# Routing inside the attention loop, scattered rows and scatter-added results in place of a sort and a dense part, and a register wait for each tile's expert weights

## What is computed

```python
x = x + tanh(g_xattn) * xattn(layernorm(x), ctx, ...)   # 16 heads of 64, one shared k and v; softmax; @Wo;
                                                        # plus silu(gate) * h @ Wff2 with h, gate = xn @ Wff1
x = x + tanh(g_ffn) * ffn(layernorm(x), ...)

# ffn: the shared expert, and the best 2 of 8 experts for each token, of width 256 and hidden size 256
shared = silu(x @ sh_up_w + sh_up_b) @ sh_down_w + sh_down_b
scores = softmax(xf @ gate_w.T)
topk_w, topk_i = top_k(scores, 2); topk_w = topk_w / (topk_w.sum() + 1e-20)
h = silu(einsum('nd,edh->neh', xf, up_w) + up_b)
y = sum over the token's two experts of topk_w * (h @ down_w + down_b)
```

## Time and profile before

| | us |
|---|---|
| runs of the kernel before | 632.3, 631.11, 632.21 (median 632.21) |
| span of the profiled execution, first to last instruction | 629.7 |
| busy in the span: PE, DVE, ACT, POOL | 550.9, 447.8, 343.6, 237.9 |

### The profile page before, as it was taken

The page is one execution under the profiler, slowest core; times in us unless marked ns, Lnnn a source line. Parts: engine busy times, 40 slices in busy tenths (PEclk is TensorE's granted clock), DMA queues, the critical chain, the costliest instruction groups (busy, mean ns, idle before and its releaser), DMA issues.

```text
span 629.7 us, 13343 instructions
## 1 busy us (share of the span) xinstructions
PE 550.9 (87%) x4099; PEld 522.0 (83%) x4100; DVE 447.8 (71%) x1176; ACT 343.6 (55%) x1108; POOL 237.9 (38%) x254
## 2 busy tenths in 40 slices
PE   1779999999999999999999999998477999995175
PEld 1778999999999999999999999987477999984175
DVE  7767878778778878778877876768997445551057
ACT  2467656756666756665766665776603444531042
POOL 3355523323323333332342342354626444127600
PEclk9989999999999999999999999999859999997568
DMA  4550200100100100000100000005202333323303
GB/s 144 164 179 30 84 2 1 36 0 0 33 0 0 33 0 0 33 0 0 33 0 0 0 17 1 2 18 168 69 18 83 119 117 115 86 75 102 108 1 133
DMA packets 26691, 31.54 MB, mean 50 GB/s; under 512 B 2947, under 2 KB 24388, under 8 KB 26660
## 3 DMA queue, kind: packets, MB, share of 16 engines
q1 hardware_dynamic: 23244, 22.88, 11.2%
q0 software_dynamic: 3088, 8.27, 4.8%
q10 hardware_dynamic: 330, 0.02, 0.0%
HBM read 22.61 MB, written 8.55 MB: 49 GB/s over the span
## 4 chain that ended last, share of the span: by engine, by line
PE 68%; DVE 15%; ACT 5%; issue 5%; another core or an unknown queue 5%; DMA 0%; DVEq 0%; POOL 0%; ACTq 0%; SPq 0%
PE bank L1325 21%; PE bank L1326 19%; PE bank L1327 19%; PE bank L1459 4%; PE bank L1522 2%; DVE xn L847 2%; ACT pr L647 1%; PE bank L1653 1%; PE bank L1645 1%; DVE acts L1018 1%; ACT acts L622 1%; DVE xs L1301 1%; ACT weights L695 1%; DVE q_t L1086 1%
## 5 line engine op out<-in xcount | busy, mean ns | idle before, releaser
L507 POOL TENSOR_TENSOR pr<-pr,rden 128x512 f32<-128x512 f32 x64 | 66.7, 1042 | 161.2 <-DVE rden L1013 161.0
L1325 PE MATMUL bank<-acts,weights 128*128 128x256 f32 x384 | 110.6, 288 | 5.8 <-DVE weights L895 2.9
L1327 PE MATMUL bank<-acts,weights 128*128 128x256 f32 x384 | 109.8, 286 | 0.0
L1326 PE MATMUL bank<-acts,weights 128*128 128x256 f32 x384 | 109.6, 286 | 0.0
L647 ACT ACTIVATE pr<-bank,nmax 128x128 f32<-128x128 f32 x256 | 90.4, 365 | 28.1 <-DVE nmax L984 27.1
L1325 PEld LDWEIGHTS bank<-acts,weights 128*128 128x128 f32 x384 | 74.8, 195 | 10.2 <-issue 4.0
L1325 PE MATMUL bank<-weights,acts 128*128 128x256 f32 x256 | 80.5, 314 | 2.1 <-POOL acts L512 2.0
L512 POOL TENSOR_TENSOR acts<-uf,acts 128x256 fp32r<-128x256 f32 x64 | 47.1, 736 | 83.1 <-ACT acts L639 83.1
L1326 PEld LDWEIGHTS bank<-acts,weights 128*128 128x128 f32 x384 | 74.5, 194 | 2.4
L955 DVE TENSOR_TENSOR acts<-bank,acts 64x256 fp32r<-64x256 f32 x128 | 53.9, 421 | 30.1 <-ACT acts L622 29.3
L1327 PEld LDWEIGHTS bank<-acts,weights 128*128 128x128 f32 x384 | 74.5, 194 | 0.0
(11 more groups left out here) (248 smaller groups left out, 1630.6 us busy)
## 6 DMA issues: line engine op xcount, KB each, us to landing
slot_rows<-stage SPq DMA_DIRECT2D x35, 128.0 KB
ct<-in_ctx SPq DMA_DIRECT2D x8, 256.0 KB, 2.7
xs<-in_x SPq DMA_DIRECT2D x8, 256.0 KB, 4.8
spare<-in_L_xattn_Wff SPq DMA_DIRECT2D x8, 256.0 KB, 4.4
norm_rows<-xn SPq DMA_DIRECT2D x7, 256.0 KB, 2.2
out_x<-xs SPq DMA_DIRECT2D x3, 512.0 KB, 3.0
stage<-in_L_xattn_Wff SPq DMA_DIRECT2D x2, 512.0 KB, 4.4
stage<-in_L_xattn_Wo SPq DMA_DIRECT2D x2, 512.0 KB, 5.0
```

The costliest lines, as they stand in the source:

```text
L507: pool.tensor_tensor(pr[:, s % 2], pr[:, s % 2], rden[:, s % 2, :].unsqueeze(2).broadcast_to((P, 4, P)), ALU.mult).then_inc(probs_ready, 1)
L1325: pe.matmul(ps, wts[1], mov[0], start=first, stop=False, skip_group_check=True)
L1326: pe.matmul(ps, wts[0], mov[0], start=False, stop=False, skip_group_check=True)
L1327: return pe.matmul(ps, wts[0], mov[1], start=False, stop=last, skip_group_check=True)
```

## The change

Routing moves into the attention loop, one group behind, for all eight groups. For each group DVE finds the best two experts (max, max_index), PE counts choices within the group (count_choices), and DVE adds running counts per expert (taken) to give each of the token's two copies a row in its expert's region of slot_rows. POOL scatters the normalised rows there, each with two more columns, the token's number and the choice's weight: first choices at the end of the iteration, second choices at s = 1 of the next but one. X1T moves from s = 5 to s = 3, GL from s = 7 to s = 5. The last group takes the same way in the bridge. SP fills 640 rows past each expert's count with pad rows in the last iteration, ahead of the last two groups' rows.

All four steps of the shared expert run before the tiles, and SP stores their sums to the output. There are 39 tiles. SP loads each with plain DMAs, its first row from a register. PE waits in each tile for ring_ready to reach the tile's expert number plus 2, a value in a register, and no longer for all splits before tile 0. DVE multiplies a tile's result by its weights, and POOL adds it to the output rows in DRAM by an indirect DMA with addition. Scatter t waits for that of t-2, and for that of t-1 where tile t has another expert or is past the last filled tile (a count from a table, in a register). The dense part, norm_rows, the stores and the fetching back go. The bias rows are no longer padded with zeros to 128 rows.

```diff
-MIX_MID = ["FF0", "QP2", "FF1", "FF2", "QP3", "FF3", "FF4", "FF5", "X1T", "TXc", "FF6", "GL", "FF7",
+MIX_MID = ["FF0", "QP2", "FF1", "FF2", "QP3", "FF3", "X1T", "FF4", "GL", "FF5", "TXc", "FF6", "FF7",
            "TXx"] + NEXT
-MIX_LAST = [n for n in MIX_MID if n not in ["TXc", "TXx"] + NEXT]
+MIX_LAST = [n for n in MIX_MID if n not in ["TXc", "TXx"] + NEXT] + ["RK"]
...
-NTS = NB - 2
-NCH = 2 * NTS
-TILES = NCH + NE - 1
+TILES = 2 * NB + NE - 1
...
@@ SP
+            for e in range(NE):
+                first = sp.value_load(start_at[0:1, e:e + 1], min_val=0, max_val=PAD_ROW - AHEAD)
+                sp.dma_start(slot_rows[bass.ds(first, AHEAD)].rearrange("(a p) n -> p a n", p=P),
+                             pad_row.unsqueeze(1).broadcast_to((P, AHEAD // P, ROW))).then_inc(pads_stored, 16)
...
+            def load_tile(t, slot_of):
+
+                row = sp.value_load(tile_row[0:1, bass.ds(t, 1)], min_val=0, max_val=PAD_ROW)
+                sp.dma_start(rows_g[:, slot_of, :], slot_rows[bass.ds(row, P), 0:D]).then_inc(gathered[slot_of], 16)
+                sp.dma_start(meta[:, bass.ds(t, 1), :].rearrange("p a n -> p (a n)"), slot_rows[bass.ds(row, P), D:ROW]
+                             ).then_inc(gathered[slot_of], 16)
...
+            sp.wait_ge(tables_done, 1)
+            sp.wait_ge(first_routed, 32 * (NG + 1))
+            sp.wait_ge(second_routed, 32 * (NG + 1))
...
@@ POOL
+            def send(rows, c, done):
+
+                for t in range(2):
+                    pool.indirect_dma_start(slot_rows[:, :], bass.IndirectOffsetOnAxis(ap=slot[:, 2 * t + c:2 * t + c + 1], axis=0),
+                                            rows[:, t, :], None).then_inc(done, 16)
+
+            def second_rows(g, rows):
+
+                pool.wait_ge(first_routed, g * 32 + 64)
+                pool.sem_inc(send_steps, 1)
+                pool.tensor_copy(rows[:, :, D + 1], w_second).then_inc(weight_moved, 1)
+                pool.wait_ge(weight_moved, g + 2)
+                pool.sem_inc(send_steps, 1)
+                send(rows, 1, second_routed)
+
+            def first_rows(g, rows):
+
+                pool.wait_ge(slots_done, g + 1)
+                pool.wait_ge(token_done, g + 2)
+                pool.sem_inc(send_steps, 1)
+                send(rows, 0, first_routed)
...
+                    if s == 1 and not first:
+                        second_rows(g - 2, xrow)
...
+            expert_lo(2)
+            second_rows(NG - 2, xrow)
+            for c in range(3, 6):
                 expert_lo(c)
-            for c in range(5, NPOS - 1):
+            pool.wait_ge(slots_done, NG)
+            send(xrow_last, 0, first_routed)
+            expert_lo(6)
+            second_rows(NG - 1, xrow_last)
+            for c in range(7, NPOS):
                 expert_lo(c)
...
+            pool.wait_ge(written, 16 * TPS)
+            for t in range(TILES):
+                pool.wait_ge(y_copied, t + 1)
+                if t >= 1:
+                    due = pool.value_load(turn[0:1, t:t + 1], min_val=16, max_val=16 * (TILES // 2 + 2))
+                    pool.wait_ge(y_added[t % 2], 16 * (t // 2) + 16)
+                    pool.wait_ge(y_added[(t - 1) % 2], due)
+                else:
+                    pool.wait_ge(y_added[0], 16)
+                    pool.wait_ge(y_added[1], 16)
+                pool.indirect_dma_start(out_rows, bass.IndirectOffsetOnAxis(ap=meta[:, t, 0:1].bitcast(I32), axis=0),
+                                        ys[:, t % 4, :], None, compute_op=ALU.add).then_inc(y_added[t % 2], 16)
...
@@ DVE
-                    if s > 1:
+                    if s > 1 or s == 0 and not first:
                         small_step()
...
+                    if s == 3 and not first:
+
+                        dve.wait_ge(second_routed, g * 32)
+                        norm_apply(call, x_tiles(g - 1), xrow[:, :, 0:D], 4, x1norm_done)
+                    if s == 4 and not first:
+                        x1_lo(g - 1, mix_ps[mix_bank("X1T", g, first, last)]).then_inc(mix_freed, 1)
...
                         dve.scalar_tensor_tensor(u1[:, :], th[:, :], 1.0, b[:, GT:2 * GT], ALU.add, ALU.mult
                                                  ).then_inc(u1_done, 1)
+                        if s == 1 or s == 2 or s == 0 and not first:
+                            small_step()
...
-                    if s in (1, 2, 3):
+                    if s in (1, 2, 3) or s == 0 and not first:
                         small_step()
...
+            def best_logits(n):
+
+                for t in range(2):
+                    done = dve.max(top[:, t, :], lgt[:, t, :])
+                done.then_inc(route_step, 1)
...
+            def token_ranks(b):
+
+                dve.tensor_tensor(rank, b[:, 0:2 * NE].rearrange("p (t e) -> p t e", t=2),
+                                  taken.unsqueeze(1).broadcast_to((P, 2, NE)), ALU.add)
+                return dve.tensor_copy(added, b[:, 2 * NE:3 * NE])
...
                     if isinstance(t, int):
+                        n, weight = t - 2, meta[:, t - 2, 1:2]
                         if t >= 6:
-                            dve.wait_ge(y_stored[b], 16 * ((t - 2) // 4))
+                            dve.wait_ge(y_added[b % 2], 16 * (n // 2))
...
-                    dve.tensor_copy(ys[:, b, :], bank[6 + c % 2][:, 0:D]).then_inc(y_copied, 1)
...
+                    dve.tensor_scalar(ys[:, b, :], bank[6 + c % 2][:, 0:D], weight, None, ALU.mult).then_inc(y_copied, 1)
...
@@ PE
+            def turn_logits(b, src):
+
+                for t in range(2):
+                    done = pe.transpose(b[:, GT + t * NE:GT + (t + 1) * NE], src[:, t * P:(t + 1) * P], ident[0:NE, 0:NE])
+                done.then_inc(lt_filled, 1)
+
+            def count_choices(b, n):
+
+                pe.wait_ge(chosen_done, n + 1)
+                pe.matmul(b[:, 0:3 * NE], before, chosen, start=True, stop=False, skip_group_check=True)
+                pe.matmul(b[:, NE:3 * NE], ones, chosen[:, 0:2 * NE], start=False, stop=False, skip_group_check=True)
+                return pe.matmul(b[:, 2 * NE:3 * NE], ones, chosen[:, 0:NE], start=False, stop=True,
+                                 skip_group_check=True)
...
+                            if i == 1 and s == 5 and not first:
+                                pe.wait_ge(lgt_done, g)
...
-                    if s == 5 and not first:
+                    if s == 3 and not first:
                         b = mix("X1T", g, first, last)
                         pe.wait_ge(x1norm_done, g)
-                        transposes(b, xn[:, 0:2]).then_inc(mix_filled, 1)
+                        transposes(b, xrow).then_inc(mix_filled, 1)
...
                 if loop is None and t == 0:
-                    for n in range(NE):
-                        split(pe, NCA + 1 + n)
                     pe.wait_ge(brow_in, 32)
-                    pe.wait_ge(windows_done, 1)
+                    pe.wait_ge(tables_done, 2)
...
                     e = pe.snap((experts_of >> (SHIFT * (k + 2))) & (NE - 1))
+                    pe.wait_ge(ring_ready, e + 2)
...
```

More of the change, by code:

```diff
@@ L581, in _ @@
+            for i in range(2):
+                pool.wait_ge(y_added[i], 16 * len(range(i, TILES, 2)) + 16)
         @block.scalar
@@ L656, in iteration @@
                         probs_hi(u - 1, first and s == 1)
+                    if s == 4 and not first:
+                        act.wait_ge(mix_filled, mix_index("X1T", g, first, last) + 1)
+                        act.activation(gates_in[:, 0:1], gates[:, 0:1], ACT.Copy)
+                        x1_hi(g - 1, mix_ps[mix_bank("X1T", g, first, last)])
                     if s < NU:
@@ L1032, in iteration @@
                                                  ).then_inc(mix_freed, 1)
-                    if s == 5 and not first:
-                        x1_lo(g - 1, mix_ps[mix_bank("X1T", g, first, last)]).then_inc(mix_freed, 1)
+                    if s == 7 and not first:
+                        choice_weights(g - 1, xrow)
                     if s == 0:
@@ L1442, in iteration @@
                         done.then_inc(mix_filled, 1)
+                    if s == 5 and not first:
+                        turn_logits(gl, lgT)
                     if s == 0:
```

900 lines of the change are left out of this document (416 added, 484 removed).

## The result

The change makes the kernel slower. The changed kernel takes 659.89 us (median of four runs, 658.63 to 663.66) where the kernel before, run beside it, takes 631.66: ratio 1.0452, 95% interval 1.0411 to 1.0494. I had forecast 607 and put 0.17 on slower. The profiled execution took 658.63, of which the span is 656.8.

The account below looks back on a forecast made before the run. PE was taken to bound the attention loop and expert tiles, DVE the bridge, nothing the dense part. From 632.2, minus 71.3, plus 17.3, 4.9, 11.3 and about 12 for the scatters' tail gave 607 us; range 583 to 636.

Parts of the forecast that it names:

- What bounds the kernel now: Whole kernel before: PE bounds attention loop and expert tiles, DVE's sorting chain the bridge, no engine the dense part.
- little slack: Attention loop: DVE and ACT form a ring of dependent work nearly as long as PE's slot.
- the 71.3 us that I booked as removed: End of the kernel before, 558.4 to 629.7: dense part and fetching back, stalled stretch included, all counted as saved.
- The attention loop, 2.5 us an iteration: Attention loop: growth per iteration from added PE work and three stalls, bounds 0.5 to 4.5, 17.3 us in all.
- The bridge, E+56: Attention to sorted tiles: tiles start 56 us after E, the end of attention, against 51.1 before; net +4.9.
- The tiles, 2.245 us each: Expert tiles: PE's pace per tile; 39 rather than 35 tiles add 9.0 us.
- the register wait: PE's ring_ready wait in each tile: 0.06 us each, 2.3 us over 39 tiles, bounds 0 and 8.
- The scatter-adds, L = 4.0: Tile stage: L is us from start to landing; 49 halves of L make a 98 us chain that binds, ending at 604.5.
- long scatters: Rival, tile stage: scatter-adds cost a read and a write in turn, L of 6.35, giving 665 us; chance 0.13.
- Slow loop: Rival, attention loop: it grows by 4.5 us an iteration, giving 621 us; chance 0.12.
- Starved code: Rival, leaving the tile loop: engines crawl during back-to-back scatter-adds, some 25 us more, giving 632 us; chance 0.08.
- PE binds: Rival, tile stage: with L under 3.6 scatter-adds keep up and PE sets the time, 596 to 599 us; chance 0.24.

Follow-up runs that it names:

- e1: The changed kernel with bias rows again zero-padded to 128 rows and full bias matmuls: 648.91 us, ratio 1.0269 to the kernel before.
- e2: The changed kernel with one constant wait for all split weights ahead of tile 0 instead of a register wait in each tile: 663.65 us, ratio 1.0485.
- e8: The kernel of e1 with plain indirect stores in place of scatter-adds, sums of shared part and experts left out of the output: 630.81 us (one run).
- e10: The kernel before with one indirect store from POOL to scratch after DVE's last addition: 612.16 us beside 606.95, ratio 1.0098.
- e9: The kernel before with only the changed kernel's two-row bias matmuls: 633.39 us beside 606.95, ratio 1.0409.
- e4: The kernel before with four unused indirect stores to scratch added to POOL in each attention iteration: 632.43 us beside 631.05, ratio 1.001.
- e13: The changed kernel with full bias matmuls, later loop steps and counting matmuls, up to four scatter-adds in flight: 624.58 us, ratio 1.0279 to the kernel before at 606.79.
- e14: The kernel of e13 with the two sends of second choices in different slots: 622.44 us, ratio 1.0251 to the kernel before at 606.79.
- e3: The changed kernel with norm steps and x1's transposes at their old places, logits one slot later, counting matmuls unmoved: 675.46 us.
- e15: The kernel before with its 32 indirect fetches at the end two at a time instead of back to back: 638.28 us beside 630.91, ratio 1.0117.

## Why the prediction was wrong

*What bounds the kernel now.* Right, and the loop's "little slack" was the reading that mattered. But the dense part's stalled stretch, among the 71.3 us that I booked as removed, is not a fixed property: at the other level the kernel before is 24 us shorter, and 19 us of PE's "issue" waits are not there. At that level the change loses 54 us, not 28.

*The attention loop, 2.5 us an iteration: mis-sized.* It grew by 5.1. Each of the three places that I named did stall: uf (0.8, and 1.1 for the pT behind it), X1T (1.9, as computed), the wait for X1T to be freed (1.0). I had the parts right and then took "one stall gives back part of the next". They added up, past even my upper bound of 4.5. My reading is that DVE starts each slot from PE's scores, so that a wait of PE delays DVE's next work too and gives it nothing back; no run shows this by itself. I had also costed nothing for the clock: in the iteration from 305.33 it was 0.97 and PE's work 51.26 us, where the one before it had 1.00 and 49.90, and so in three of seven. Over the loop, 38.3 us came where 17.3 were forecast (7 x 2.5 is 17.5; a slip of no weight).

*The bridge, E+56: right* (56.5). After it I counted 6 us to the first scatter-add. It was 10.3, at a granted clock of 0.66, with PE busy in 10.36 of 10.40 us: I had priced the first tile at the full clock.

*The tiles, 2.245 us each: the step that left something out, and the main one that failed.* I read in the diff that the bias rows are no longer padded, and costed nothing for it. It is 0.38 us a matmul, 78 times here, and puts PE at 2.86 us a tile. In the changed kernel PE and the scatter-adds are nearly equal bounds: PE is busy 103.85 of 104.90 us, though the chain without PE's delay takes 108 of the 113.8 (e1). That is why e1 gives 10 us and not the 30 that 78 times 0.38 would be. For the register wait I allowed 2.3 us; e2 shows none.

*The scatter-adds, L = 4.0: a part left out.* I had L from start to landing, and that was sized well: 3.6 to 3.8 us. But each step of the chain also holds the 0.75 us from the landing to POOL's next issue, which I had put at nothing, so a step is 4.41 to 4.62. The count of halves holds from first to last issue: e1's chain is 48 of them at 2.25. I had counted 49 to the landing of the last, which gave that landing half an L (2.0 us); it took 3.6. So the 19.5 us too many from the first scatter-add to the last landing are 12.0 of the longer step, 5.8 of PE's late tiles and some 1.6 of that landing.

The Trainium skill's figure (DMA: Bandwidth & Descriptors, "Anatomy of one DMA — SWDGE (gpsimd) path") gave an estimate of 2.3 for such a DMA, and I had put the issue on top, 3.55. From start to landing e8's last plain store took 2.40 us (619.60 to 622.00), near the 2.3 with nothing on top; an addition, of which the section doesn't speak, took 3.6 to 3.8. The rival of long scatters decides from 5.0, so it was not the cause.

*The end: left out.* I added 2.5 for what lies around the span and nothing within it. POOL now ends last, and its drain of 6.5 us stands at the end of the span, where the kernel before had it beside other work (e10).

*The rivals.* "Slow loop" was nearest, and its 4.5 too small. "Starved code" didn't come: in the tile stage PE has no "issue" wait worth a row. "PE binds" came half true, through a cost that I hadn't seen, and on the wrong side: I had it as the faster case. For "long scatters" I had named L above 5 as the sign that the prediction is wrong; it stayed under that, and the prediction failed without it. The change for the worse came from terms that I held for small and of one sign each, and my range added none of them to another.

## What to carry to other kernels

Where every engine's slot is nearly as long as PE's, a step moved earlier is a wait for each thing that now isn't ready, and the waits add; move the whole chain, or let PE meet it later. Don't shorten the contracted rows of a matmul that stands between full ones without looking at the gaps beside it: 126 rows of zeros were faster than none. A scatter-add is a latency wherever order matters, so count the places that need order first, and only then the rate. And look at which engine's program ends last: its closing instructions are in the time.

## What the runs showed of the hardware

- A matmul with 2 stationary rows between ones with 128 costs 0.38 us more than a full one at the full clock, in three gaps (0.21, 0.30, 0.23 for 0.12 each), and the 102 of e9, 70 of them in the tiles, cost 24.8 us (22.2 to 27.4). Its weight load and the next one's start with their matmuls, where those between full matmuls start 0.12 us ahead.
- A scatter-add of 128 rows of 1 KB takes POOL 1.56 us to issue, 3.6 to 3.8 from start to landing and 4.4 to 4.6 from start to start of a dependent one; a plain scattered store 0.96, 2.40 and 3.16.
- Four software sends an iteration beside a PE-bound loop cost nothing measurable (e4); in the loop of the changed kernel two of them back to back cost some 0.5 us an iteration (52.2 us in e13, 51.7 in e14).
- The granted clock stayed at 1.00 in all seven iterations of the loop before (in six of them PE worked 49.2 to 49.3 of some 49.7 us) and was 0.94 or 0.97 in six of the seven of e3 (waits of 5.7 us in 57.36). What brings it down was not tested by itself.
- POOL's program closes with a drain of 5.5 us (e10) to 6.5 us (the changed kernel). Where POOL ends last, the span goes on for 6.4 to 7.2 us after the last packet; where SP's plain store is last, under 1.
- Back-to-back indirect fetches went with PE slowed to a matmul each 1.4 us and more, on some occasions and not on others, on the same chip; with the fetches two at a time the stalls were gone (e15).
